# Joining two moving blocks in an expert's second product, and other matmul widths for small experts

## The reference

```python
x = x + 0.5 * ffn(layernorm(x), gate, wi, wo)
x = x + attn(layernorm(x), ...)
x = x + 0.5 * ffn(layernorm(x), gate, wi, wo)

def ffn(inputs, gate_weight, wi, wo):          # 8 experts, C = 320
    top1 = argmax(tokens @ gate_weight.T)
    ranks = cumsum(one_hot(top1, 8)) - 1       # place of a token in its expert
    mask = one_hot(top1, 8) * (ranks < C)      # an expert keeps its first 320 tokens
    dispatch = ...                             # the rows of each expert
    hmid = gelu(einsum('ech,ehi->eci', dispatch, wi))   # 512 -> 2048
    eout = einsum('eci,eih->ech', hmid, wo)             # 2048 -> 512
    out = ...                                  # each row back to its token, times its probability
```

## Time and profile before

| what | value |
|---|---|
| median of 3 runs | 1098.69 us (1098.29 to 1100.72) |
| span of the profiled execution, first to last instruction | 1094.0 us |
| median minus span | 4.7 us |
| TensorE busy | 1046.3 us (96%) |
| VectorE busy | 720.6 us (66%) |
| ScalarE busy | 543.8 us (50%) |
| mean granted TensorE clock | 0.983 of full speed |

### The profile page before, as it was taken

One profiled execution on the slowest core, in us unless ns is written; L12 is line 12 of the kernel. 1 busy time (PEld: TensorE's weight loads), 2 busy tenths in 40 slices (PEclk: granted clock), 3 DMA queues, 4 the chain that ended last, 5 costly groups with the idle time before them and its releaser, 6 DMA issues.

```text
span 1094.0 us, 20943 instructions
## 1 busy us (share of the span) xinstructions
PE 1046.3 (96%) x7924; PEld 988.2 (90%) x7924; DVE 720.6 (66%) x1089; ACT 543.8 (50%) x851; POOL 144.0 (13%) x138
## 2 busy tenths in 40 slices
PE   9699999999999999599999996999999999999995
PEld 6599999999999999478777776999999999999995
DVE  8556565776577686478786765557777777665552
ACT  5445455565556565253342324455665656554441
POOL 3201111203021110100000022002212021120101
PEclk9899999999999999899999998999999999999998
DMA  8568546566464761500011235436566575664410
GB/s 309 176 242 302 187 171 216 183 219 206 162 232 160 251 208 39 178 1 1 1 39 39 79 116 176 154 117 244 206 228 211 190 244 188 230 208 145 164 39 25
DMA packets 83276, 177.32 MB, mean 162 GB/s; under 512 B 4192, under 2 KB 4704, under 8 KB 83168
## 3 DMA queue, kind: packets, MB, share of 16 engines
q1 hardware_dynamic: 75488, 152.61, 40.5%
q0 software_dynamic: 7168, 23.07, 5.9%
q10 hardware_dynamic: 576, 1.05, 0.3%
HBM read 162.04 MB, written 18.87 MB: 165 GB/s over the span
## 4 chain that ended last, share of the span: by engine, by line
PE 91%; DVE 3%; DMA 2%; issue 1%; ACT 1%; POOL 1%; POOLq 0%; SPq 0%; ACTq 0%; DVEq 0%
PE psH L1223 13%; PE psH L1222 13%; PE psH L1224 13%; PE acc L1230 12%; PE acc L1231 12%; PE acc L1229 12%; PE acc L1222 3%; PE acc L1223 3%; PE acc L1224 3%; PE psT L1446 1%; PE acc L1402 1%; PE psH L1402 1%; DVE row_stats L829 1%; PE psT L1551 1%; PE psT L1281 1%
## 5 line engine op out<-in xcount | busy, mean ns | idle before, releaser
L1222 PE MATMUL psH<-dth,wih 128*128 128x240 f32 (+5 forms) x1024 | 294.3, 287 | 0.0
L1223 PE MATMUL psH<-dtl,wih 128*128 128x240 f32 (+5 forms) x1024 | 293.4, 287 | 0.8 <-issue 0.8
L1230 PE MATMUL acc<-htl,woh 128*128 128x240 f32 (+5 forms) x1024 | 293.3, 286 | 0.0
L1231 PE MATMUL acc<-hth,wol 128*128 128x240 f32 (+5 forms) x1024 | 293.1, 286 | 0.0
L1224 PE MATMUL psH<-dth,wil 128*128 128x240 f32 (+5 forms) x1024 | 293.1, 286 | 0.0
L1229 PE MATMUL acc<-hth,woh 128*128 128x240 f32 (+5 forms) x1024 | 293.1, 286 | 0.0
L796 DVE TENSOR_TENSOR wol<-raw_wo,woh 128x1024 fp32r<-128x1024 f32 x128 | 155.6, 1222 | 146.6 <-ACT woh L613 146.6
L647 ACT ACTIVATE gel<-psH 128x320 f32<-128x320 f32 x256 | 112.1, 438 | 189.1 <-PE psH L1224 183.9
L613 ACT ACTIVATE woh<-raw_wo 128x1024 fp32r<-128x1024 f32 x128 | 134.2, 1056 | 132.2 <-PE acc L1231 132.1
L1223 PEld LDWEIGHTS psH<-dtl,wih 128*128 128x128 f32 x1024 | 193.0, 188 | 1.1 <-issue 1.1
L1222 PEld LDWEIGHTS psH<-dth,wih 128*128 128x128 f32 x1024 | 192.9, 188 | 0.4
(11 more groups left out here) (194 smaller groups left out, 1147.9 us busy)
## 6 DMA issues: line engine op xcount, KB each, us to landing
raw_wi<-in_wi SPq DMA_DIRECT2D x64, 1024.0 KB, 5.1
raw_wo<-in_wo SPq DMA_DIRECT2D x64, 1024.0 KB, 5.5
out_x<-xt SPq DMA_DIRECT2D x4, 1024.0 KB, 5.9
xt<-in_x SPq DMA_DIRECT2D x6, 512.0 KB, 8.0
xt<-x SPq DMA_DIRECT2D x3, 1024.0 KB, 10.2
raw_u<-in_wuT SPq DMA_DIRECT2D x1, 1024.0 KB, 10.9
raw_u<-in_wvT SPq DMA_DIRECT2D x1, 1024.0 KB, 12.6
xt<-in_x ACTq DMA_DIRECT2D x2, 256.0 KB, 3.6
```

The lines of the kernel that those rows point to most:

```text
L1222: pe.matmul(out, lh, rh, start=first, stop=False)
L1223: pe.matmul(out, lh, rl, start=False, stop=False)
L1230: pe.matmul(out, lh, rl, start=False, stop=False, skip_group_check=True)
L1231: return pe.matmul(out, ll, rh, start=False, stop=False, skip_group_check=True)
```

## The change

`WIDTHS` becomes 192, 240, 256, 272, 288, 320: there is a body of 192 columns, and the one of 304 is gone. In bodies of up to 256 columns (`JOINT`) the two matmuls that have `woh` as weights become one, whose moving operand is the block of `hth` and the block of `htl` side by side, with its result in two regions of the bank: `hth` by `woh` from column 0 on, `htl` by `woh` from column 256 on. For that the two live in one tensor `ht`. The product with `wol` still adds onto the first region. So in a joined body `mm2` has 16 matmuls in place of 24. The two regions have to be added at the end of each expert: ACT copies the bank as before (now `eoT_copied`), and DVE adds the second region to `eoT`, times a factor `joint_now` that is 1 for a joined expert and 0 for another; PE waits for that (`eoT_sum`). DVE does this for every expert.

```diff
-WIDTHS = range(240, CAP + 1, 16)
+WIDTHS = (192, 240, 256, 272, 288, 320)
+JOINT = 256
...
-        hth = put("hth", [P, 2, ICS, CAP], F32R)
-        htl = put("htl", [P, 2, ICS, CAP], F32R)
+        ht = put("ht", [P, 2, ICS, 2, CAP], F32R)
+        hth, htl = ht[:, :, :, 0, :], ht[:, :, :, 1, :]
...
-            pool.iota(least[:, :, :], [[0, E], [WIDTHS.step, NW - 1]], base=WIDTHS.start, channel_multiplier=0,
-                      allow_small_or_imprecise_dtypes=True).then_inc(pool_const, 1)
+            for k, w in enumerate(WIDTHS[:-1]):
+                ins = pool.memset(least[:, :, k:k + 1], float(w))
+            ins.then_inc(pool_const, 1)
...
                         act.wait_ge(s.acc_done, DC * (PAIRS * e + PAIRS) + c + 1)
-                        act.activation(eoT[:, c, :], acc[c][:, 0:CAP], copy).then_inc(s.eoT_done, 1)
+                        act.activation(eoT[:, c, :], acc[c][:, 0:CAP], copy).then_inc(s.eoT_copied, 1)
...
+                then(dve.tensor_scalar(joint[:, :], ps_taken, JOINT + 0.5, None, ALU.is_lt))
...
-            for bank in (*acc[2:], *psH):
+                then(dve.tensor_copy(joint_now[:, 0:1], joint[:, 0:1]))
+                settle()
+
+            dve.memset(nil[:, :], 0.0)
+            for bank in acc[:2]:
+                dve.memset(bank[:, JOINT:], 0.0).then_inc(banks_set, 1)
+            for bank in acc[2:]:
+                dve.memset(bank[:, :], 0.0)
+            for bank in psH:
...
+                    dve.tensor_copy(joint_now[:, 1 - a:2 - a], joint[:, bass.ds(e + 1, 1)])
...
+                    for c in range(DC):
+                        dve.wait_ge(s.acc_done, DC * (PAIRS * e + PAIRS) + c + 1)
+                        dve.wait_ge(s.eoT_copied, DC * e + c + 1)
+                        dve.scalar_tensor_tensor(eoT[:, c, 0:JOINT], acc[c][:, JOINT:], joint_now[:, side:side + 1],
+                                                 eoT[:, c, 0:JOINT], ALU.mult, ALU.add).then_inc(s.eoT_sum, 1)
                     if not last:
                         for c in range(DC):
                             tokens(e + 1, c)
...
-            def onto(out, lhs, rhs):
-
-                (lh, ll), (rh, rl) = lhs, rhs
-                pe.matmul(out, lh, rh, start=False, stop=False, skip_group_check=True)
-                pe.matmul(out, lh, rl, start=False, stop=False, skip_group_check=True)
-                return pe.matmul(out, ll, rh, start=False, stop=False, skip_group_check=True)
+            def onto(bank, w, lhs, both):
+
+                lh, ll = lhs
+                if w <= JOINT:
+                    pe.matmul(bank.rearrange("p (r q) -> p r q", r=2)[:, :, 0:w], lh, both[:, :, 0:w],
+                              start=False, stop=False, skip_group_check=True)
+                else:
+                    for r in range(2):
+                        pe.matmul(bank[:, 0:w], lh, both[:, r, 0:w], start=False, stop=False, skip_group_check=True)
+                return pe.matmul(bank[:, 0:w], ll, both[:, 0, 0:w], start=False, stop=False, skip_group_check=True)
...
+                pe.wait_ge(banks_set, 2)
...
-                        pe.matmul(acc[c][:, 510:512], ones[:, :], ones[:, 0:2], start=True, stop=True)
+                        pe.matmul(acc[c][:, 510:512], ones[:, :], nil[:, :], start=True, stop=True)
...
-                        pe.wait_ge(s.eoT_done, DC * e + c + 1)
+                        pe.wait_ge(s.eoT_sum, DC * e + c + 1)
```

More of the change, by code:

```diff
@@ L138, in build_kernel @@
         digit = put("digit", [P, E], F32)
+        joint = put("joint", [P, E], F32)
+        joint_now = put("joint_now", [P, 2], F32)
+        nil = put("nil", [P, 2], BF16)
         code8 = put("code8", [P, E], F32)
@@ L258, in __init__ @@
                 self.acc_done = sem(f"acc_done{n}")
-                self.eoT_done = sem(f"eoT_done{n}")
+                self.eoT_sum = sem(f"eoT_sum{n}")
+                self.eoT_copied = sem(f"eoT_copied{n}")
                 self.tokT_done = sem(f"tokT_done{n}")
@@ L537, in _ @@
                 act.sem_inc(s.gelu_done, ICS)
-                act.sem_inc(s.eoT_done, DC)
                 def norm(g, rstd_sem, xn_sem, tiles=GROUP):
@@ L962, in _ @@
                 dve.sem_inc(s.out_dve, 3)
+                dve.sem_inc(s.eoT_sum, DC)
                 if n == 0:
@@ L1289, in logits @@
                             pe.wait_ge(gates_set, 1)
-                            pe.wait_ge(banks_set, 1)
+                            pe.wait_ge(banks_set, 3)
                         else:
@@ L1431, in mm2 @@
                             d = slice(c * P, (c + 1) * P)
-                            ins = onto(acc[c][:, 0:w], (woh[:, k, j, d], wol[:, k, j, d]),
-                                       (hth[:, k, j, 0:w], htl[:, k, j, 0:w]))
+                            ins = onto(acc[c][:, :], w, (woh[:, k, j, d], wol[:, k, j, d]), ht[:, k, j])
                         if k == 1:
@@ L1459, in turn_last @@
                     for c in range(DC):
-                        pe.wait_ge(s.eoT_done, DC * E + c + 1)
+                        pe.wait_ge(s.eoT_sum, DC * E + c + 1)
                         for k, bank in HELD:
```

## The result

The changed kernel takes 1113.55 us (median; 1112.35 to 1115.55), and the kernel before 1098.49 (1093.06 to 1100.72) over its runs, those beside the changed kernel among them. The ratio of the two is 1.0159, 95% interval 1.0136 to 1.0182, which is 17.5 us; the medians lie 15.1 us apart. It was forecast at 1093.2, and it is slower.

A forecast was written before the change was run, and what follows sets the result against it. PE, busy 96% of the span, was taken as the bound, by matmul start distances. Bodies -10.7 us and boundary additions +5.2 gave -5.5: span 1094.0 to 1088.5, plus 4.7 around it, 1093.2 us; range 1087 to 1098.

The forecast's parts named there:

- The rest, at nothing: DVE's split into `ht`, larger clears, `joint_now`, POOL clears and DMA: each claimed to cost nothing, being hidden or unchanged.
- The sum it did make: Matmul savings in the bodies, -10.7 us, plus delays at the boundaries from DVE's additions, +5.2 us: together -5.5 us.
- the price by columns: Matmul start distance in proportion to width, 0.46 ns a column: 88 ns for a single matmul of 192 columns.
- the floor of the weight load: Each narrow matmul's own load of 128 weight columns bounds it at 110 to 113 ns; taken as 112, so `mm1` gains nothing.
- The first rival: Weight loads don't bound at 192 columns: single matmuls cost 88 ns, 24 us gained in four bodies, about 1070 to 1078; chance 0.04.
- the second (bf16 rate, 161 + 112): Joined matmuls run at the bf16 warm-up's rate, 15 to 19 ns less each, 9.7 us in all: about 1084; chance 0.06.
- The additions: DVE at each expert's end: four of about 0.41 us, 0.38 apart, 1.5 us together; boundary delays sum to +5.2 us.
- one delay: At a boundary, PE's wait for the first addition and late `dtl` coincide: 0.4 us behind 240, 0.73 behind 192.
- The fourth rival: Slower: a 256-column addition on DVE costs 0.73 us, boundary delays reach 22.6 us, result 1110; chance 0.06.
- The fifth: The expert with count 191 routes differently and runs at 240 columns, so 3.1 us stay away: 1096; chance 0.04.
- The third: No change: joined matmuls at their upper price, boundaries at 7.5 us, small losses before `mm2`: 1097.5 to 1100.5; chance 0.10.
- The prediction's other sign of being wrong: A body of 240 columns taking longer than the 384 x 112 = 43 us of before would make the prediction wrong.

## Why the prediction was wrong

**The step that failed** is the one headed "The rest, at nothing". It lists the split, the clears, `joint_now`, DMA and queues, and it has no term for the code: six bodies in another order, the first of them unused in layer 1, with PE branching among them. The earlier trace rows had the place for such a cost, "issue 1%", and the page 27 packets of instructions; the branch, the `visit` blocks and their padding are in the kernel. None of the five rivals has it. The prediction's own last sentence named the sign, a new wait that none of them names; it had given slower a chance of 0.06, and all of that to the additions. What the runs showed in its place: six waits of PE for code, 16.6 us of idle time and some 4.7 more of lower clock and slow starts behind them, five of which go when the unused body is put last in layer 1 (1113.55 to 1094.03 us).

**The sum it did make** holds, as the rows of after show: not only the total but the prices behind it came out. Some of the exactness is luck, since a body of 240 gained 0.2 us more than forecast and a wide boundary lost 0.1 more.

Timeline of PE, `mm2` in a body of 192:

```profile
868.16 0.36 PE L1249 MATMUL acc<-ht,woh 128*128 128x384 f32 x1
868.36 0.25 PE L1254 MATMUL acc<-ht,wol 128*128 128x192 f32 x1
868.44 0.36 PE L1249 MATMUL acc<-ht,woh 128*128 128x384 f32 x1
```

- A pair there takes 286 ns, predicted 288. The split of it is another: 198 from the joined to the `wol` matmul and 88 from that to the next, where 176 and 112 were predicted. The 88 is the price by columns that the prediction gave for 192. The rest of the load's price seems to have moved in front of the long matmul: that is a reading of the starts, which no run tests. The two still add up. At 480 + 240 columns the pair takes 221 + 106 = 327 (predicted 331.5), at 512 + 256 349 (354; 360 before).
- Single matmuls of 192 columns in `mm1` are at the floor of the weight load, as predicted:

```profile
869.52 0.27 PE L1243 MATMUL psH<-dth,wil 128*128 128x192 f32 x1
869.63 0.27 PE L1241 MATMUL psH<-dth,wih 128*128 128x192 f32 x1
869.74 0.28 PE L1242 MATMUL psH<-dtl,wih 128*128 128x192 f32 x1
```

  111 ns apart. The first rival (88) and the second (bf16 rate, 161 + 112) are refuted.
- A body of 192 takes 40.7 to 40.8 us up to the next boundary's first transpose. 0.65 of that is the wait for the first addition, counted from start to start as below, so 40.1 in place of 43.08: a gain of 2.9 to 3.0, predicted 3.1. There are some 0.3 us of short waits in it, most of them where PE goes from `mm1` of a to `mm1` of b in the last pass (0.33 and 0.19 us between starts in place of 0.11). 304 to 320 costs 56.39 - 52.99 = 3.4, predicted 3.2.
- The additions: 478 ns each, four in 1.65 us, 0.39 apart (predicted 0.41 and 0.38). By form, DVE of after, and the end of a body of 192:

```profile
L1083 DVE SCALAR_TENSOR_TENSOR eoT<-acc,joint_now,eoT 128x256 f32<-128x256 f32 x64 | 27.8, 478 | 7.7 <-ACT eoT L685 7.5
```

```profile
844.84 1.23 DVE L801 TENSOR_TENSOR wol<-raw_wo,woh 128x1024 fp32r<-128x1024 f32 x1 [0.35 <-ACT woh L618]
845.98 1.65 DVE L1083 SCALAR_TENSOR_TENSOR eoT<-acc,joint_now,eoT 128x256 f32<-128x256 f32 x4
847.57 0.89 DVE L801 TENSOR_TENSOR dtl<-acc,dth 128x320 fp32r<-128x320 f32 x2
```

  On PE there:

```profile
846.52 0.94 PE L1426 MATMUL acc<-ident,dn 128*128 128x128 f32 x6 [0.48 <-DVE eoT L1083]
...
848.91 0.25 PE L1432 MATMUL acc<-nil,ones 128*128 128x2 bf16 x4
```

  The wait for the first addition and the lateness of `dtl` are one delay, as the prediction argued. Its size is not the idle time of 0.48, because a matmul's duration reaches past the place where the next could have started: behind 192 the first transpose starts 0.74 to 0.78 us after the last matmul, behind 240 0.46 to 0.52, and in before 0.115. The clear then comes 0.06 later after that transpose than in before. So the delay is 0.65 + 0.06 = 0.70 behind 192 (predicted 0.73), 0.40 behind 240 (0.4), and 0.13 behind wide bodies (0.05). A period at 192 went from 45.93 to 43.7, so -2.2 net; the prediction's is -3.07 + 0.73 = -2.34. Without the delay a body of 240 gained 0.47 (predicted 0.29). The period at 240 changed by -0.07 (predicted +0.11), that at 256 by -0.57.
- The split into `ht` with gaps costs nothing: the groups of after are at 495 and 826 ns.

```profile
L1046 DVE CAST ht<-gel 128x640 fp32r<-128x640 f32 x128 | 63.3, 495 | 101.2 <-ACT gel L652 99.8 <-issue 0.8
...
L801 DVE TENSOR_TENSOR ht<-gel,ht 128x640 fp32r<-128x640 f32 x128 | 105.7, 826 | 4.4
```

The fourth rival ended at 1110, near the result, by a mechanism that isn't there: its additions of 0.73 us are 0.48. The fifth is refuted by the four bodies of 192. The third needs the upper prices; those measured are near the forecast's or below.

Two slips of the prediction change nothing of this. By the N/2.4 + 2.5 ns of the Trainium skill (TensorE: Matmul & The Clock Gate, section Back-to-back issue gap) the three joined matmuls take 162.5, 202.5 and 216 ns, as an estimate, and that is 9 us better than the sum, not "some 7". And the weight loads at 192 are not "halved": a group goes from three to two.

The prediction's other sign of being wrong, a body of 240 that takes longer than 43 us, came true as well (44.16 and 44.01 us), through the lower clock behind the waits.

**What stays open.** How many pieces PE holds and which one it gives up; why a wait is 2 us in one place and 3.4 in another; why the second 288 waits without visits. Nor is it known why the kernel before itself spreads from 1092.5 to 1102.0 us over the runs of this study, which is more than the whole forecast gain; and with such a spread the profiled execution, one of the runs, can differ by some microseconds from the median.

## What to carry to other kernels

Where an engine branches among several long bodies, as PE does here, the code can be a resource with a price: before adding a body, or changing the order of those there are, list which of them each loop really runs, and try the unused ones behind the used ones. In a profile look at the packets of the instruction queue and at idle time put down to `issue` on the first instruction after a branch; between the layouts here with 27 to 29 packets and those with 39 lay 15 to 23 us. A wait can hide under another name: the row of before that named `DVE dtl` was one for code. And a profile that shows none of this today says nothing of the next layout. And a body for a narrow case pays only if what it saves isn't bounded by something else: 192 columns alone gained 0.14 us in 43, and only making one matmul of the two that load the same weights gained 2.8 more.

## What the runs showed of the hardware that was not expected

- A branch of PE to another body can stop it for 1.8 to 3.4 us while packets of instructions arrive (the waits at the clear in all changed layouts here; 1.1 in the kernel before), also where it ran that body two or four bodies earlier (240 and 288 in layer 1 of after).
- Behind four of the six stops of after it ran at the lower of its two clock levels for 3.4 us: a granted clock of 0.60 over the 3.9 us behind the one at 164 us. In the layouts with 192 second and third the body of 272 behind its wait takes 50.61 and 50.59 us in place of 48.21, with no further wait in it and 6.8 us at the lower level, so the second cost (2.4 us) can come near the first (2.9 and 3.4).
- A short matmul can start closer behind a long one than among its equals: 88 ns from a 192-column matmul to the next start behind a 384-column one, 111 among equals. The Trainium skill (TensorE: Matmul & The Clock Gate, section LDWEIGHTS) has P/1.2 ns for a load, 107 for 128 columns; the runs agree nearly with 111 among single matmuls of 192 columns. The 88 lie below both; the sum of the pair (286) stays at the 176 + 112 of the separate prices.
- A moving operand of two blocks with a gap, and a result in two regions of a bank, cost nothing over one block: 480 columns take 221 ns and 512 take 232, where one block of 512 took 234.
